# A 512-step recurrence on one core: scores also with keys on partitions, products of x in bulk through DRAM, and no products of ones

## What is computed

```python
def step(h, x_t):
    proj = h @ W
    score = jnp.einsum('bsh,bh->bs', enc_hiddens, proj)
    attn = jax.nn.softmax(score, axis=-1)
    context = jnp.einsum('bs,bsh->bh', attn, enc_hiddens)
    inp = jnp.concatenate([x_t, context], axis=-1)
    gx = inp @ kernel + bias
    gh = h @ recurrent_kernel
    ...
    z = jax.nn.sigmoid(xz + hz)
    r = jax.nn.sigmoid(xr + hr)
    cand = jnp.tanh(xh + r * hh)
    h_new = z * h + (1.0 - z) * cand
```

## Time and profile before

| | |
|---|---|
| median of three runs | 3,068.23 us (3,067.42 to 3,076.98) |
| profiled execution: time, span | 3,084.98 us, 3,082.8 us |
| busy share of the span | PE 88%, DVE 70%, ACT 56%, POOL 32% |
| mean granted TensorE clock | 0.97 |
| recurrence, first to last state scan | 1003.12 to 2961.72 us |
| TensorE busy, 2514.00 to 2521.00 | 5.27 of 7.00 us, granted clock 1.00 |
| TensorE busy, 2700.00 to 2714.00 | 11.31 of 14.00 us, granted clock 1.00 |
| a load of weights, issue to landing | 2.3 us (64 KB), 3.0 us (256 KB) |
| four loads back from a DRAM scratch (576 KB each) | 6.3 us |

### The profile page before, as it was taken

One profiled execution on the slowest core, in us unless ns is written; L12 is line 12 of the kernel. 1 busy time (PEld: TensorE's weight loads), 2 busy tenths in 40 slices (PEclk: granted clock), 3 DMA queues, 4 the chain that ended last, 5 costly groups with the idle time before them and its releaser, 6 DMA issues. The chain is left out here.

```text
span 3082.8 us, 131006 instructions
## 1 busy us (share of the span) xinstructions
PE 2726.5 (88%) x54163; PEld 1797.8 (58%) x54163; DVE 2146.9 (70%) x8143; ACT 1713.6 (56%) x5762; POOL 997.4 (32%) x1992
## 2 busy tenths in 40 slices
PE   7999999888778999899999899999989888888769
PEld 4666666575455555565566566666656545444439
DVE  5666666773432888788888688888878766777653
ACT  4666666533443666576776576666657544333322
POOL 2000000231110566355766355555535311000015
PEclk9999999999878999999999999999999999999989
DMA  4000000000011000000001010000001000000013
GB/s 142 5 5 7 5 6 5 11 1 1 19 30 42 7 14 31 4 31 17 11 10 31 4 44 4 11 7 11 28 3 33 8 4 3 4 3 4 3 45 80
DMA packets 41077, 56.47 MB, mean 18 GB/s; under 512 B 6238, under 2 KB 27688, under 8 KB 40360
## 3 DMA queue, kind: packets, MB, share of 16 engines
q1 hardware_dynamic: 36392, 42.46, 4.4%
q0 software_dynamic: 4096, 5.67, 1.0%
HBM read 42.45 MB, written 5.67 MB: 16 GB/s over the span
## 5 line engine op out<-in xcount | busy, mean ns | idle before, releaser
L2183 POOL TENSOR_TENSOR gru_terms<-gru_states,gru_signs 128x8 f32<-128x8 f32 x512 | 104.2, 204 | 1147.5 <-DVE gru_states L2470 1043.5
L2103 ACT ACTIVATE gru_p<-gru_ps_sg,gru_negmax 128x78 f32<-128x78 f32 x512 | 167.6, 327 | 331.1 <-DVE gru_negmax L2439 326.3
L2107 ACT ACTIVATE gru_th_r<-gru_pre_r 128x32 f32<-128x32 f32 x512 | 119.4, 233 | 406.6 <-DVE gru_pre_r L2450 406.6
L1691 PE MATMUL gru_ps_sg<-ctx_gate_w,gru_p_t 128*4 128x64 f32 x12288 | 267.3, 220 | 0.1
L368 ACT ACTIVATE self_probs<-self_sc,self_negmax 128x512 f32<-128x512 f32 x256 | 174.4, 685 | 166.1 <-DVE self_negmax L425 166.1
L2159 POOL TENSOR_SCALAR bg_probs<-bg_probs,bg_arsum 128x256 f32<-128x256 f32 (+2 forms) x192 | 241.0, 1255 | 19.0
L1936 PE MATMUL gru_ps_sg<-score_w,gru_states 128*4 128x78 f32 x4096 | 165.1, 234 | 74.2 <-DVE gru_states L2470 73.0
L2439 DVE TENSOR_REDUCE gru_negmax<-gru_ps_sg 128x1 f32<-128x78 f32 x512 | 121.8, 238 | 146.9 <-PE gru_ps_sg L1936 142.3
L2443 DVE STREAM_TRANSPOSE gru_p_t<-gru_p 128x96 f32<-128x96 f32 x512 | 142.7, 279 | 112.7 <-ACT gru_p L2103 112.5
L1940 PE MATMUL gru_ps_own<-late,gru_states 128*4 128x128 f32 x4096 | 208.4, 276 | 0.0
L1691 PEld LDWEIGHTS gru_ps_sg<-ctx_gate_w,gru_p_t 128*4 128x4 f32 x12288 | 172.2, 86 | 38.3 <-issue 0.3
(11 more groups left out here) (421 smaller groups left out, 7302.4 us busy)
## 6 DMA issues: line engine op xcount, KB each, us to landing
bg_w<-in_moe_w SPq DMA_DIRECT2D x48, 256.0 KB, 3.0
bg_wa<-in_wqkv SPq DMA_DIRECT2D x24, 192.0 KB, 2.3
moe_w<-in_moe_w SPq DMA_DIRECT2D x16, 256.0 KB, 2.9
best_w_sb<-in_ec_w SPq DMA_DIRECT2D x16, 256.0 KB
cross_scratch<-ctab_raw SPq DMA_DIRECT2D x16, 154.0 KB
cross_outs<-cross_scratch POOLq DMA_DIRECT2D x4, 576.0 KB, 6.3
late<-in_late SPq DMA_DIRECT2D x1, 2269.5 KB
self_w_sb<-in_wqkv SPq DMA_DIRECT2D x8, 192.0 KB, 2.3
```

Of the source, the lines that this page charges most:

```text
L1691: last = pe.matmul(bank[32 * c:32 * c + B, 0:hi - lo], p_t[:, 32 * k:32 * k + B], gate_w[:, k, 96 * c + lo:96 * c + hi], start=k == 0, sto ...
L2103: act.activation(p[:, 0:CTX + 1], ps_s[:, 0:CTX + 1], ACT.Exp, bias=negmax[:, 0:1], accum_out=total[:, 0:1])\
```

## The change

- The scores are made twice. Once as before, for the maximum, but each product now has the state's column broadcast to 32 stationary columns, so that all 32 rows of a group hold the same scores, with no mask. And 12 products with `score_w` stationary (32 keys each) and the state moving (4 columns), on top of a mask product: keys on partitions, 12 columns. ACT exponentiates these (128x12) straight into `p_t`; the transpose on DVE, the sum on ACT and the spreading products are gone.
- The total is two more columns of `gate_w` (34 instead of 32 for r). Gate products are now r with the total (34 columns), then candidate and z together (64 columns), in 98 columns per chunk. The reciprocal follows the r products; `pre_r` follows it; candidate and z are one DVE step.
- The products of x for 120 of each tile's 128 steps are made in bulk, one product per batch, copied by ACT, stored to DRAM by SP and loaded back for eight steps at a time with the right rows; DVE adds them while taking the own products. The other eight steps of a tile make them as before.
- All products of ones are removed.
- The background work has new places: other stages for the units (a turn of q and k into its own bank, four buffers of v, two of turned probabilities for all tiles), tangent a step earlier, `hidden` in halves before and after the maximum, one quarter of `down` and a few more products ahead of the gate products (`ahead_of_gates`), everything else behind them (`after_gates`). Tile starts move: attention 0, 110, 219; experts 76, 186, 330 (before 0, 114, 226 and 79, 193, 335). SP's loads are issued at steps of their own.
- Constants no longer used in the recurrence stand at the end of their tile, and their room (`spare`) holds the rows of x products; 2,560 columns of it are cleared at the start.

```diff
-                dve.scalar_tensor_tensor(out=gate_w[:, k, :], in0=bias_rows, scalar=is_key[:, k:k + 1],
-                                         in1=ps[1 + k][:, 0:3 * P], op0=ALU.mult, op1=ALU.add)
-
-
-def recurrence(nc, x_t, score_w, gate_w, h_w, x_w, mask_l, mask_r, spread, h0_t, later):
+                by_chunk = gate_w[:, k, :].rearrange("p (c g) -> p c g", c=4)
+                bias = bias_rows.rearrange("p (c g) -> p c g", c=4)
+                product = ps[1 + k][:, 0:3 * P].rearrange("p (c g) -> p c g", c=4)
+                dve.scalar_tensor_tensor(out=by_chunk[:, :, 0:32], in0=bias[:, :, 0:32], scalar=is_key[:, k:k + 1],
+                                         in1=product[:, :, 0:32], op0=ALU.mult, op1=ALU.add)
+                dve.scalar_tensor_tensor(out=by_chunk[:, :, GATE_C:GATE_ALL], in0=bias[:, :, 32:96], scalar=is_key[:, k:k + 1],
+                                         in1=product[:, :, 32:96], op0=ALU.mult, op1=ALU.add)
+                dve.tensor_copy(by_chunk[:, :, 32:GATE_C], is_key[:, k:k + 1].rearrange("p (a b) -> p a b", a=1).broadcast_to([P, 4, 2]))
...
+        STAGES = {2: {"project": 0, "squares": 0, "take_v": 1, "sums": 1, "rows": 2, "turn": 2, "take_qk": 2, "scores": 3,
+                      "max0": 4, "exp0": 4, "scale0": 4, "max1": 5, "exp1": 5, "scale1": 5, "probs0": 5, "turned0": 5, "probs1": 6, "turned1": 6,
+                      "values": 6, "take_out": 7, "out": 7, "add": 8},
+                  3: {"project": 0, "squares": 0, "take_v": 1, "sums": 1, "rows": 2, "turn": 4, "take_qk": 4, "scores": 4,
+                      "max0": 5, "exp0": 5, "scale0": 5, "max1": 6, "exp1": 6, "scale1": 6, "probs0": 6, "turned0": 6, "probs1": 8, "turned1": 8,
+                      "values": 11, "take_out": 11, "out": 12, "add": 13}}
...
+            GATING[g] = ATTENTION[g] + PACE[g] * (U - 1) + (9 if PACE[g] == 2 else 13)
+            EXPERTS[g] = GATING[g] + 5
+        ADDING = 8
...
+        def from_rows(t):
+
+            return t % P >= CHUNK
...
+            def store_rows(g, b, n):
+                sp.wait_ge(s_xrow, n + 1)
+                sp.dma_start(x_products[g * P + CHUNK:(g + 1) * P, b, :], x_rows[0:P - CHUNK, :, :].rearrange("p c g -> p (c g)")).then_inc(s_xout, 16)
+
+            def load_rows(k):
+                sp.wait_ge(s_xout, 16 * B * (k * CHUNK // P + 1))
+                sp.wait_ge(s_own, (k - 1) * CHUNK)
+                for b in range(B):
+                    sp.dma_start(x_in[b:P:32, k % 2, :, :], x_products[k * CHUNK:(k + 1) * CHUNK, b, :].rearrange("t (c g) -> c t g", c=4))\
+                      .then_inc(s_xin[k % 2], 16)
...
-                                         gate_w[:, k, 96 * c + lo:96 * c + hi], start=k == 0, stop=k == 2,
+                        last = pe.matmul(bank[32 * c:32 * c + B, 0:hi - lo], p_t[:, B * k:B * k + B],
+                                         gate_w[:, k, GATE_ALL * c + lo:GATE_ALL * c + hi], start=k == 0, stop=k == 2,
...
+            def x_rows_of(g, b, n):
+                pe.wait_ge(s_own, BULK[g] + b + 1)
+                wait_positive(pe, s_xt, g)
+                pe.matmul(ps_x[0:P - CHUNK, :], x_t[:].rearrange("p (t b) -> p b t", b=B)[:, b, g * P + CHUNK:(g + 1) * P], x_w.rearrange("p c g -> p (c g)"),
+                          start=True, stop=True).then_inc(s_xmm, 1)
...
+            def ahead_of_gates(t):
                 for g, n, m in chunks_at(t, 4):
-                    down(g, n, m, 1)
-                    busy = True
+                    down(g, n, m, range(1))
                 for g, n, m in units_at(t, "turn"):
-                    turn_qk(g, n, m)
-                    busy = True
-                for j in range(2):
-                    for g, n, m in units_at(t, f"probs{j}"):
-                        turn_probs(g, n, m, j)
-                        busy = True
-                for at, g in gating_at(t, 9):
-                    turn_gates(at, g)
-                    busy = True
-                for at, g in gating_at(t, 10):
-                    gate_biases(at, g, 1)
-                    busy = True
-                if not busy:
-                    wait_positive(pe, s_prez, t)
-                    fill_in(2 * P, ps_tz)
-
-            def before_scores(t):
-                busy = False
+                    if PACE[g] == 3:
+                        turn_qk(g, n, m)
+                for g, n, m in units_at(t, "out"):
+                    if PACE[g] == 3:
+                        project_out(g, n, m)
+                for g, n, m in units_at(t, "probs1"):
+                    if PACE[g] == 2:
+                        turn_probs(g, n, m, 1)
+
+            def after_gates(t):
...
             pe.wait_ge(s_init, n_init)
             for t in range(S):
                 if t:
-                    pe.wait_ge(s_own, t)
-                wait_positive(pe, s_xt, t // P)
-                for c in range(4):
-                    pe.matmul(ps_own[32 * c:32 * c + B, 0:96], x_t[:, B * t:B * (t + 1)], x_w[:, c, :], start=True, stop=False,
-                              tile_position=(0, 32 * c), skip_group_check=True)
-                busy = t and before_scores(t - 1)
-                wait_positive(pe, s_u, t)
-                pe.matmul(ps_s[:, 0:CTX + 1], mask_l, mask_r[:, 0:CTX + 1], start=True, stop=False, skip_group_check=True)
-                if not busy:
-                    wait_positive(pe, s_prez, t)
-                    for i in range(6):
-                        fill_in(2 * P, ps_tz)
+                    after_gates(t - 1)
+                wait_positive(pe, s_own, t)
+                if not from_rows(t):
+                    wait_positive(pe, s_xt, t // P)
+                    for g, b, n in bulk_at(t - 1):
+                        pe.wait_ge(s_xrow, n + 1)
+                    for c in range(4):
+                        pe.matmul(ps_own[32 * c:32 * c + B, 0:96], x_t[:, B * t:B * (t + 1)], x_w[:, c, :], start=True, stop=False,
+                                  tile_position=(0, 32 * c), skip_group_check=True)
+                wait_positive(pe, s_precz, t)
+                pe.matmul(ps_t, mask_l, mask_r, start=True, stop=False, skip_group_check=True)
                 pe.wait_ge(s_h, t + 1)
                 for b in range(B):
-                    last = pe.matmul(ps_s[32 * b:32 * b + B, 0:CTX + 1], state(t), score_w[:, b, 0:CTX + 1], start=False, stop=True,
-                                     tile_position=(0, 32 * b), skip_group_check=True)
+                    last = pe.matmul(ps_s[32 * b:32 * b + 32, :], state(t)[:, b:b + 1].broadcast_to([P, 32]), score_w[:, b, 0:CTX + 1],
+                                     start=True, stop=True, tile_position=(0, 32 * b))
                 last.then_inc(s_score, 1)
+                for k in range(3):
+                    for b in range(B):
+                        last = pe.matmul(ps_t[32 * b:32 * b + 32, B * k:B * k + B], score_w[:, b, 32 * k:32 * k + 32], state(t),
+                                         start=False, stop=True, tile_position=(0, 32 * b), skip_group_check=True)
+                last.then_inc(s_turnedmm, 1)
+                for g, b, n in bulk_at(t - 1):
+                    pe.wait_ge(s_xrow, n + 1)
                 for c in range(4):
-                    last = pe.matmul(ps_own[32 * c:32 * c + B, 0:P], state(t), h_w[:, c, :], start=False, stop=True,
+                    last = pe.matmul(ps_own[32 * c:32 * c + B, :], state(t), h_w[:, c, :], start=from_rows(t), stop=True,
                                      tile_position=(0, 32 * c), skip_group_check=True)
                 last.then_inc(s_ownmm, 1)
-                after_own(t)
+                ahead_of_gates(t)
                 pe.wait_ge(s_exp, t + 1)
-                for c in range(4):
-                    last = pe.matmul(ps_t[32 * c:32 * c + B, 0:2], spread, total[:], start=True, stop=True, tile_position=(0, 32 * c))
-                last.then_inc(s_total, 1)
-                pe.wait_ge(s_own, t + 1)
-                fill_in(P, ps_own)
-                pe.wait_ge(s_pt, t + 1)
-                gate_products(ps_g, 0, 64).then_inc(s_rcmm, 1)
-                pe.wait_ge(s_rt, t + 1)
-                gate_products(ps_z, 64, 96).then_inc(s_zmm, 1)
+                gate_products(ps_r, 0, GATE_C).then_inc(s_rmm, 1)
+                gate_products(ps_cz, GATE_C, GATE_ALL).then_inc(s_czmm, 1)
...
-                act.activation(p[:, 0:CTX + 1], ps_s[:, 0:CTX + 1], ACT.Exp, bias=negmax[:, 0:1], accum_out=total[:, 0:1])\
-                   .then_inc(s_exp, 1)
+                act.wait_ge(s_turnedmm, t + 1)
+                act.activation(p_t[:], ps_t, ACT.Exp, bias=negmax[:, 0:1]).then_inc(s_exp, 1)
                 after_exp(t)
                 act.wait_ge(s_prer, t + 1)
                 act.activation(th_r[:, 1:64:2], pre_r[:], ACT.Tanh, scale=0.5).then_inc(s_thr, 1)
-                act.wait_ge(s_prez, t + 1)
-                act.activation(th_z[:], pre_z[:], ACT.Tanh, scale=0.5).then_inc(s_thz, 1)
```

(90 more changed lines are left out.)

282 lines of the change are left out of this document (147 added, 135 removed).

## The result

The changed kernel is slower: 3,097.0 us median of 4 runs (3,093.9 to 3,101.6) against 3,071.5 (3,067.4 to 3,077.0, also 4 runs: one more than stood in the table), a ratio of 1.0079 with a 95% interval of 1.0060 to 1.0098. The prediction was 2,988 us in a range of 2,895 to 3,070, with a chance of 0.83 on faster. The time lies above the range, and the kernel is slower by 0.8%.

A forecast was written before the change was run, and what follows sets the result against it. The prediction took the recurrence's ring of hand-overs to bound the kernel, TensorE's list in busy steps afterwards. Step groups of 1,845 us plus additions made 1,882, 80 less; 3,005 times 0.9946 gave 2,988 us, range 2,895 to 3,070.

The forecast's parts named there:

- Busy steps: Steps with background work: full clock, TensorE's list between gates and next scores the longer way; expert steps 3.50 us each.
- POOL's argument before; no bound of their own: Expert steps: ACT's unit input and tangent end at about 3.4 us, POOL's argument earlier, so neither sets the step.
- What would show it: Signs in the trace: late light steps at clock 0.5 from step 366, scores waiting for TensorE in expert steps.
- light steps: Steps without background work: 163 x 3.80 us = 619 at the low clock, 3.26 at the full clock.
- the prediction's additions: Added to 1,845 us: norms and choices 12, expert starts 9, bulk products 6, clearing and tables 3, clock dips 3, first step 4.
- The clock: Without products of ones, light steps drop from 2.4 to 1.2 GHz and cost 3.80 us instead of 3.26.
- Busy attention steps: Attention units, bound by TensorE's list: tile 1 3.46 us, tile 2 3.78 (7.56 for two), tile 3 3.38 a step.
- the queueing rival: New score products: loads of 32 columns queue, taking 0.72 us instead of 0.18; 3,275 us in all; chance 0.09.
- The DRAM round: Storing x products and loading them for eight steps at a time costs nothing; without that cover, 4 us stalls 60 times.
- The sum: Recurrence: 512 steps 1,845 us, with additions 1,882, against 1,958.6 + 3.8 before: 80 us less.
- the last factor of 0.9946: Whole kernel: 3,005 us scaled from the profiled execution to the median of runs, giving 2,988 us.
- the four rivals: Clock stays up (0.08), busy steps fall to the ring's 3.3 us (0.12), loads queue (0.09), low clock in busy stretches (0.05).

The follow-up runs named there:

- experiment 1: Changed kernel with r's tanh kept in PSUM instead of SBUF: 3,024.4 us, 0.9822 of the kernel before.
- experiment 2: Changed kernel with POOL's product of 128x512 issued as two of 128x256: 3,060.3 us, 0.9930 of the kernel before.
- experiment 3: Changed kernel with POOL's product of two tensors replaced by a multiplication of one tensor by 0.5: 3,042.6 us, 0.9890 of the kernel before.
- experiment 6: Changed kernel with POOL's gelu argument and ACT's tangent one step later, as in the kernel before: 3,015.8 us, 0.9811 of the kernel before.
- experiment 7: Kernel before with only POOL's gelu argument moved one step earlier: 3,141.7 us, 1.0225 of the kernel before.
- experiment 8: experiment 1 with the state scan's factors in PSUM too: 3,007.9 us, 0.9792 of the kernel before.
- experiment 4: Changed kernel with eight products of ones back in each step without background work: 3,015.4 us, 0.9785 of the kernel before.
- experiment 5: Kernel before without its products of ones: 3,192.2 us, 1.0383 of the kernel before.
- experiment 9: experiment 8 with eight products of ones in each step without background work, ahead of the mask's product: 2,927.4 us, 0.9519 of the kernel before.

## Why the prediction was wrong

**The step that failed** stands under "Busy steps", experts: "POOL's argument before; no bound of their own", and with it 103 x 3.50 = 361. I asked only when POOL and ACT would be done, not what DVE does meanwhile. The sign named under "What would show it", that in expert steps the scores wait for TensorE, failed too: TensorE waited 0.85 for DVE's state. An expert step took 4.48, and the three expert stretches 452 us. Experiments 1 to 3 and 6 to 8 show the cause: the scan is held by POOL's operation for as long as that runs. Of the 103 us, 78 scans of about 1.40 make 78 x 1.11 = 87, and five shorter ones beside the product 2. The other 15 lie beside POOL's scaling in attention steps, mostly of tile 1 and 2, and cost little: two tile 2 steps take 3.50 + 4.06 = 7.56 with the hold and 3.77 + 3.80 = 7.57 without (experiment 1), both TensorE's 7.56 of the prediction.

The Trainium skill says it ("SBUF — State Buffer", on who interferes with whom and in the summary of rules): a VectorE instruction with two inputs in SBUF contends with a GpSimd instruction that reads SBUF, and whichever comes second blocks until the first is over. Here the trace agrees for the product and for experiment 3, with 0.13 to 0.15 us more after the end; the prediction didn't weigh it. In the trace of before POOL's product and the scan never met. But three of its 512 scans did run beside POOL's scaling and took 0.58, 0.40 and 0.36, so the hold could be seen there:

```profile
1462.32 1.26 POOL L2159 TENSOR_SCALAR bg_probs<-bg_probs,bg_arsum 128x384 f32<-128x384 f32 x1
1462.46 0.58 DVE L2459 TENSOR_TENSOR_SCAN gru_c_in<-gru_th_r,gru_own 128x64 f32<-128x64 f32 x1
```

The earlier trace rows names the scan's two inputs.

From scan to scan by the prediction's own groups of steps, measured and (in brackets) predicted: experts 452 us (361), light steps 635 (619), tile 1 242 (242), tile 2 272 (265), tile 3 376 (358), together 1,977 (1,845). The excess of 132 is 91 in the experts and 41 elsewhere, of which the prediction's additions had foreseen 33. In experiment 8, without the hold, the experts take 374.

**The clock.** Right: 0.5 from step 366 to the end but for some short stretches before 2,562 us; light steps 3.30 at the full clock (predicted 3.26), 3.91 at the low one (3.80). Of the 0.11, gates to scan took 1.62 for 1.55, exponential to gates 0.33 for 0.27 (the exponential of 128x12 itself 0.27 for 0.22, at either clock), scores to exponential 0.89 for 0.86. About 155 x 0.11 = 17 us. Experiment 4 puts the clock's price at 82 us in the new ring; of the 118 us of experiment 5, 80 to 94 are the clock's in the old one.

**Busy attention steps.** 3.46, 3.78 and 3.38 predicted for tiles 1, 2 and 3; 3.46, 3.78 and 3.38 measured as means over two, two and three steps of the settled pattern. That is closer than the 0.1 either way that the prediction gave itself, so partly luck. Over the whole stretches, with starts, norms and dips of the clock, tile 2 takes 3.89 a step and tile 3 3.55. Experts without the hold: 3.58 for 3.50, 8 us in all.

**The new products** take 0.35 with their tail at the full clock, as expected from the earlier trace rows (0.18 + 0.19), and 0.50 at the low one; the queueing rival is false. **The DRAM round** is never waited for: wherever DVE's additions of the loaded rows (L2502) wait, it is for TensorE's own products. **The sum** without the hold: experiment 8, at the same low clock, takes 1,889 us from the first scan to the last, against 1,878 predicted, and 3,008 us against 3,005 before the last factor of 0.9946. That factor was wrong to apply: it corrected for one profiled execution, and later sets have the kernel before at 3,071 to 3,078. So one missing mechanism (about 89 us of median, experiment 8), 17 us of this factor and 3 of the rest make up the 109. The 3 is a balance: the recurrence was 11 above the prediction, and the parts around it came out shorter than in the profile of before.

None of the four rivals came true, and none of them had the hold. That the products of ones pay in the new ring too (experiment 9 against 8: 80 us) was foreseen as a price and not as advice.

## What to carry to other kernels

When work moves in time on one of POOL and VectorE, list what the other does in that stretch, and look for VectorE instructions with two inputs in SBUF: here the scan stood still whenever it came second to POOL's product, up to 1.40 us instead of 0.29. Keep one input of the critical one in PSUM, or place the long operation between. A kernel whose TensorE turns lighter can lose by the clock what it gains by the lighter work; price both rings at both levels before taking work out.

## What was not expected of the hardware

The hold does not always last as long as POOL's operation. Scaling of probabilities (one tensor, the scale one number per partition) in the changed kernel:

```profile
1584.12 1.25 POOL L2220 TENSOR_SCALAR bg_probs<-bg_probs,bg_arsum 128x384 f32<-128x384 f32 x1
...
1584.28 0.56 DVE L2516 TENSOR_TENSOR_SCAN gru_c_in<-gru_th_r,gru_own 128x64 f32<-128x64 f32 x1
```

The scan ends 0.72 behind POOL's start and 0.53 ahead of its end. The Trainium skill's rule ("SBUF — State Buffer", summary of rules) that the second blocks until the first finishes would make it 1.2 long. It is regular: beside scalings of 128x256, 128x384 and 128x512 (0.93, 1.25 and 1.58 us long) the long scans end 0.32, 0.53 and 0.74 ahead of POOL's end. The scan's second input in SBUF is behind this too: with r's tanh in PSUM (experiment 1) no scan beside a scaling is longer than 0.29. Why this form lets go sooner wasn't tried. A VectorE instruction may also delay POOL's (0.82 for 0.72, experiment 2). And the granted clock stayed at 0.50 although TensorE was busy for 232 of 360 us from 2600 on, and never idle for more than 1.14 us.
